# Hyena block with a gated FFN: gated values of twelve halves turned by way of memory and VectorE instead of TensorE

## Chip, cores and metric

One core of a Trainium2 chip runs the whole program. The metric is device time in microseconds, a median over runs; the profile is of one execution.

## The reference

Eight sequences of 512 positions with 512 features pass a long-convolution (Hyena) layer with a post-layernorm, then a gated FFN with quantised weights and a second post-layernorm.

```python
u = x @ in_proj_w.T + in_proj_b                      # (8, 512, 1536)
uc = short_conv(u, 3 taps, causal) + short_b         # per channel
x0, x1, v = split(uc, 3)                             # 512 channels each
v = v * x1                                           # the gated values
y = fftconv(v, k, filter_bias) * x0                  # long filter k from a small sine MLP
x = layernorm(x + y.T @ out_proj_w.T + out_proj_b)
h = silu(x @ Wg.T) * (x @ Wu.T)                      # 1408 hidden
out = layernorm(x + h @ Wd.T)
```

## The kernel before

The work is cut into 16 halves: half `n` is 256 of the 512 channels of sequence `n // 2` in the convolution part, and 256 of its 512 positions in the FFN part. The program is a software pipeline. Each round `n` has eleven beats (0 to 10), and in one round the engines work on the input projection (`ip`), short convolution (`conv`) and gating (`v1`) of half `n`, on the spectra and products of half `n-1` (`fw`, `mul`, `acc`, `iv`), on the output projection of half `n-2` (`op`, `ln1`), and on one FFN unit of 128 hidden features per beat (`gu`, `silu`, `hmul`, `hhi`, `hlo`, `dn`). A steady round takes about 60 us, a beat about 5.5 us. `beat_steps` writes the steps of a beat as a list, and every engine, SyncE with its DMA queue included, walks the same list in the same order and does its own part of each step. So each queue is strictly in order: an instruction that waits holds all that is behind it on its engine.

What the change and the prediction touch:

- **Gated values.** `v1` (GpSimd, L778) multiplies `cv` by `cx1` into `cv[:, c, :]`, channels on partitions, for channel blocks c = 0 and 1. In beats 7 and 8 the step `tv` (TensorE, L1094, four 128x128 products with the identity each) turns them to positions on partitions, into a PSUM bank; `vsplit` in the beat after copies the bank to `vT_hi` (ScalarE) and subtracts for `vT_lo` (VectorE, L899). `fw` of the next round reads both.
- **The ring of two banks.** `ip`, `tv`, `iv` and `op` take the two PSUM banks by turns. Each waits until the reader of the second last use is through. The second output projection of a round, `("op", n-2, 1)` in beat 7, takes the bank of the first one, which VectorE's `ln1` (L932) reads; `ln1` of beat 7 also waits for GpSimd's `resid` (L808).
- **SyncE's queue.** Beat 5: loading a block of down weights (`wdload`, L557), storing two blocks of the output (`store`, L623), and reloading `x` into their place (`resload`, L636), which waits until the stores have landed. In beats 1, 3, 5 and 7 of even rounds `xload` (L524) fetches a block of the next sequence in squares: four DMAs of 64 KB with runs of 128 bytes. VectorE turns these 32x32 squares (`xturn`, L863) in beats 2 to 5 of odd rounds. Beat 10: four DMA transposes (L614) from `parts` to `x2T_hi` and `x2T_lo`; `gu` of beat 2 in the next round waits for them.

Of the kernel before, what the change touches and what calls it, by code (L numbers as in the profile page):

```python
# [5 lines left out]
P = 128  # L6
NSEQ, L, D = 8, 512, 512
HID = 1408
TB = L // P
# [4 lines left out]
HALVES = 2 * NSEQ  # L14
# [44 lines left out]
BY_SQUARES = range(2, NSEQ)  # L59
SQUARE = 32  # L60


def shared(n, beat):

    ips, out, steps = n < HALVES, 0 <= n - 2 < HALVES, []
    if beat == 0 and 0 <= n - 3 < HALVES and n - 3 not in BY_DMA:
        steps += [("x2t", n - 3, 0), ("x2t", n - 3, 1)]
    if beat in (6, 7) and out:
        steps += [("op", n - 2, beat - 6)]
    if beat in PROJECTION_OF_BEAT and ips:  # L70
        steps += [("ip", n, *PROJECTION_OF_BEAT[beat])]
    if beat in (7, 8) and ips and n not in (1, 2):
        steps += [("tv", n, beat - 7)]
    if beat == 6 and n in (1, 2):
        steps += [("tv", n, 0), ("tv", n, 1)]
    if beat == 1 and out:
        steps += [("iv", n - 2, 3)]
    if beat in INVERSE_OF_BEAT and 1 <= n <= HALVES:
        steps += [("iv", n - 1, INVERSE_OF_BEAT[beat])]
    if beat in (9, 10) and n % 2 == 1 and n + 1 < HALVES and (n + 1) // 2 not in BY_SQUARES:  # L80
        steps += [("xt", (n + 1) // 2, 2 * (beat - 9) + b) for b in range(2)]
    return steps
# [15 lines left out]
def beat_steps(n, beat):  # L98
# [68 lines left out]
        steps += [("var", LN1, n - 2)]  # L167
    if beat in (9, 10):
        steps += readers([p for p in shared(n, beat) if p[0] == "xt"])
    following = (n + 1) // 2  # L170
    if n % 2 == 1 and following in BY_SQUARES:
        if beat in (2, 3, 4, 5):
            steps += [("xturn", following, beat - 2)]
        if beat in (7, 8, 9, 10):
            steps += [("xsplit", following, beat - 7)]
    if beat == 10 and n - 2 in BY_DMA:
# [128 lines left out]
def build(nc, x, win, wout, wg, wu, wd, fwd, shifted, inv, decay, z_pos, w0, w1, w2, w3, net_cols, fbias,  # L305
          conv_w, conv_cols, gate_cols, up_cols, down_row, out_row, identity, out):
    ctx = ExitStack()
    with ctx:
# [3 lines left out]
        def sem(name):  # L312
            return ctx.enter_context(nc.semaphore(name))
# [46 lines left out]
        spectrum = [ctx.enter_context(nc.psum_tensor(f"spectrum{n}", [P, 2, W], F32)) for n in range(2)]  # L360
        bank = [ctx.enter_context(nc.psum_tensor(f"bank{n}", [P, D], F32)) for n in range(2)]

        wd_scratch = nc.dram_tensor("wd_scratch", (HID, D), F32).ap()

        ident_in, consts_in, taps_in, late_in, decay_in = (sem(f"{n}_in") for n in ("ident", "consts", "taps", "late", "decay"))
# [21 lines left out]

        x_hi_done, x_lo_done, x_turned = sem("x_hi_done"), sem("x_lo_done"), sem("x_turned")
        tap2_done, tap1_done, v1_done = sem("tap2_done"), sem("tap1_done"), sem("v1_done")
        v_hi_done, z_hi_done, z_lo_done = sem("v_hi_done"), sem("z_hi_done"), sem("z_lo_done")  # L390
        res_biased, x2_hi_done, x2_lo_done = sem("res_biased"), sem("x2_hi_done"), sem("x2_lo_done")

# [10 lines left out]
        def flat(ap):  # L403
            return ap.rearrange("p a b -> p (a b)")
# [91 lines left out]
        def turned_block(kb):  # L496

            return xstage[:, kb - 1, :] if kb else turned[:, :]

        def by_dma(m):  # L500

            return min(max(m - BY_DMA[0], 0), len(BY_DMA))
# [7 lines left out]
        def _(sp):  # L510
# [77 lines left out]
            for kind, *at in steps:  # L588
# [8 lines left out]
                elif kind == "wdload":  # L597
                    m, q = at
                    index = HB * m + q
                    for n in ((0, 1, 2) if index == 0 else (index + 2,)):  # L600
                        if n < HB * HALVES:
                            load_down(n)
                elif kind == "x2dma":
                    m, = at
                    if m == BY_DMA[0]:
# [35 lines left out]
        def _(act):  # L641
# [13 lines left out]
            for kind, *at in steps:  # L655
# [29 lines left out]
                elif kind == "conv":  # L685
# [1 line left out]
                    q = COLS[t] * CB + 2 * (n % 2) + c  # L687
                    k = use["ip", n, c, t]
                    act.wait_ge(bank_ready, k + 1)
                    if t == V and n > 0:  # L690
                        act.wait_ge(bank_ready, use["tv", n - 1, 1] + 1)
                    elif t == X1:
                        act.wait_ge(v1_done, 2 * n + c)
                    elif t == X0 and n == 1:
                        act.wait_ge(filt_mm, 2 * TB)
                    elif t == X0 and n >= 2:
                        act.wait_ge(z_lo_done, TB * (n - 1))
# [6 lines left out]
                    last.then_inc(tap2_done, 1)  # L704
                elif kind == "vsplit":
                    n, jp = at
                    k = use["tv", n, jp]
                    act.wait_ge(bank_ready, k + 1)
                    if n > 0:
                        act.wait_ge(spectrum_ready, TB * (n - 1) + 2 * jp + 2)  # L710
                    A(flat(vT_hi[:, 2 * jp:2 * jp + 2, :]), bank_of(k), ACT.Copy).then_inc(v_hi_done, 1)
                elif kind == "z":
                    n, i = at
                    act.wait_ge(*read_of(use["iv", n, i]))
# [25 lines left out]
                elif kind == "x2part":  # L740
                    m, b = at
                    act.wait_ge(ln_done[LN1], 2 * m + b + 1)
                    if m > BY_DMA[0]:
                        act.wait_ge(x2t_in, 64 * by_dma(m))
                    A(parts[:, b, 0, :], row_tile(m, b), ACT.Copy).then_inc(x2_hi_done, 1)
# [74 lines left out]
        def _(dve):  # L820
# [5 lines left out]
            for kind, *at in steps:  # L826
# [55 lines left out]
                elif kind == "conv":  # L882
# [9 lines left out]
                    dve.wait_ge(tap1_done, number + 1)  # L892
                    STT(out=dst[:, 2:], in0=src[:, :L - 2], scalar=taps[:, q, 0:1], in1=dst[:, 2:],  # L893
                        op0=ALU.mult, op1=ALU.add).then_inc(bank_read[bank_index[k]], 1)
                elif kind == "vsplit":
                    n, jp = at
                    k = use["tv", n, jp]
                    dve.wait_ge(v_hi_done, 2 * n + jp + 1)
                    TT(flat(vT_lo[:, 2 * jp:2 * jp + 2, :]), bank_of(k), f32(flat(vT_hi[:, 2 * jp:2 * jp + 2, :])),  # L899
                       ALU.subtract).then_inc(bank_read[bank_index[k]], 1)  # L900
                elif kind == "mul":
# [101 lines left out]
        def _(pe):  # L1003
# [18 lines left out]
            for kind, *at in steps:  # L1022
# [74 lines left out]
                elif kind == "fw":  # L1097
                    n, j = at
                    k = TB * n + j
                    pe.wait_ge(*read_of(use["tv", n, j // 2]))  # L1100
                    if k >= 2:
                        pe.wait_ge(made_done, made["mul", n - (j < 2), (j + 2) % 4, 3, 1] + 1)
                    else:
# [133 lines left out]
```

## Time and profile before

| | us |
|---|---|
| median of 3 runs (lowest, highest) | 1011.18 (1010.74, 1011.89) |
| the profiled execution's own time | 1010.81 |
| its span | 1009.0 |
| PE busy | 988.4 |
| DVE busy | 733.8 |
| POOL busy | 570.6 |
| ACT busy | 425.8 |

The span runs from the first to the last instruction of the program; 1.8 us of the execution's time lie around it. PE is TensorE, DVE is VectorE, ACT is ScalarE, POOL is GpSimd, SPq is SyncE's queue, which issues the DMAs.

### The profile page before, as it was taken

How to read it: one execution, taken by the hardware profiler on the slowest of the kernel's cores; microseconds unless marked ns; L12 is line 12 of the kernel's file. 1: busy time of each engine (PE TensorE's matmuls, PEld its weight loads, DVE VectorE, ACT ScalarE, POOL GpSimd, SP SyncE). 2: the span in 40 equal slices, each digit the busy share in tenths (PEclk: the TensorE clock that was granted, in tenths of full speed). 3: DMA queues.
4: the chain of work that ended last, by engine and by line, in shares of the span. 5: the costliest groups of instructions: out<-in, count | busy, mean ns of one | idle time of the engine just before them, and what ended most of it. 6: DMA issues, size and time to landing. Idle time of an engine off the chain costs nothing.

```text
span 1009.0 us, 17595 instructions
## 1 busy us (share of the span) xinstructions
PE 988.4 (98%) x6214; PEld 803.3 (80%) x6214; DVE 733.8 (73%) x1338; ACT 425.8 (42%) x929; POOL 570.6 (57%) x628
## 2 busy tenths in 40 slices
PE   8999999999999999999999999999999999999996
PEld 5578788888888888888888888788888888888885
DVE  5598867868777787776878677876877777686454
ACT  4675434433343434434343343443334343434342
POOL 4599663756547465564647546465654746575210
PEclk9999999999999999999999999999999999999999
DMA  8674423242243413434223422424223231323332
GB/s 250 198 223 130 106 63 91 72 105 59 84 95 94 95 43 95 87 91 96 89 58 85 105 74 84 90 67 109 62 84 84 85 68 49 95 74 105 117 115 73
DMA packets 125883, 97.02 MB, mean 96 GB/s; under 512 B 83040, under 2 KB 87776, under 8 KB 125796
## 3 DMA queue, kind: packets, MB, share of 16 engines
q1 hardware_dynamic: 125298, 95.83, 35.3%
q8 instruction: 50, 0.82, 0.3%
q14 instruction: 37, 0.30, 0.1%
q10 hardware_dynamic: 498, 0.08, 0.0%
HBM read 78.30 MB, written 11.27 MB: 89 GB/s over the span
## 4 chain that ended last, share of the span: by engine, by line
PE 72%; DVE 13%; issue 6%; ACT 5%; SPq 2%; POOL 1%; DMA 1%; POOLq 0%; ACTq 0%; DVEq 0%
PE gate_up L1159 12%; PE gate_up L1160 12%; PE bank L1010 9%; PE bank L1012 9%; PE bank L1011 9%; PE down L1170 6%; PE down L1171 6%; PE bank L1119 4%; DVE tmp L917 2%; DVE hid_lo L1000 2%; ACT cx L702 2%; DVE cx L890 2%; ACT x L727 1%; PE bank L1094 1%; DVE cx L893 1%
## 5 line engine op out<-in xcount | busy, mean ns | idle before, releaser
L791 POOL TENSOR_TENSOR acc<-acc,tmp 128x256 f32<-128x256 f32 x160 | 123.0, 769 | 147.2 <-DVE tmp L917 135.1
L917 DVE TENSOR_TENSOR tmp<-spectrum,filt 128x512 f32<-128x512 f32 x256 | 173.0, 681 | 0.4 <-PE spectrum L1012 0.4
L755 ACT ACTIVATE hid<-gate_up,gate_scale 128x256 f32<-128x256 f32 x176 | 82.8, 471 | 197.6 <-PE gate_up L1160 196.5
L1159 PE MATMUL gate_up<-x2T_hi,wg_sb 128*128 128x256 f16 x704 | 165.0, 275 | 1.0 <-DMA x2T_lo<-parts 1.0
L1159 PE MATMUL gate_up<-x2T_hi,wu_sb 128*128 128x256 f16 x704 | 163.3, 273 | 0.0
L1160 PE MATMUL gate_up<-x2T_lo,wg_sb 128*128 128x256 f16 x704 | 163.2, 273 | 0.0
L1160 PE MATMUL gate_up<-x2T_lo,wu_sb 128*128 128x256 f16 x704 | 163.2, 273 | 0.0
L785 POOL TENSOR_TENSOR acc<-acc,tmp 128x512 f32<-128x512 f32 x96 | 126.4, 1317 | 48.5 <-DVE tmp L917 48.0
L1010 PE MATMUL bank<-xT_hi,win_hi 128*128 128x512 f32 x360 | 148.4, 412 | 0.8 <-POOL win_lo L773 0.6
L1170 PE MATMUL down<-wd_sb,hid_hi 128*128 128x512 f32 x352 | 148.7, 422 | 0.4 <-DVE hid_lo L1000 0.2
L1011 PE MATMUL bank<-xT_lo,win_hi 128*128 128x512 f32 x360 | 142.3, 395 | 0.0
L1012 PE MATMUL bank<-xT_hi,win_lo 128*128 128x512 f32 x360 | 142.1, 395 | 0.0
L1171 PE MATMUL down<-wd_sb,hid_lo 128*128 128x512 f32 x352 | 139.1, 395 | 0.0
L994 DVE SCALAR_TENSOR_TENSOR hid<-gate_up,up_scale,hid 128x256 f32<-128x256 f32 x176 | 84.4, 480 | 73.3 <-ACT hid L755 72.6
L1000 DVE TENSOR_TENSOR hid_lo<-hid,hid_hi 128x256 fp32r<-128x256 f32 x176 | 114.9, 653 | 28.5 <-ACT hid_hi L762 28.5
L762 ACT ACTIVATE hid_hi<-hid 128x256 fp32r<-128x256 f32 x176 | 73.6, 418 | 135.4 <-DVE hid L994 131.7
L792 POOL TENSOR_TENSOR acc<-acc,tmp 128x256 f32<-128x256 f32 x160 | 119.9, 749 | 0.0
L702 ACT ACTIVATE cx<-bank,conv_bias,taps 128x1 f32<-128x1 f32 x186 | 78.1, 490 | 95.9 <-PE bank L1012 92.6
L1159 PEld LDWEIGHTS gate_up<-x2T_hi,wg_sb 128*128 128x128 bf16 x704 | 68.5, 97 | 51.4 <-issue 43.6
L890 DVE SCALAR_TENSOR_TENSOR cx<-bank,taps,cx 128x511 f32<-128x511 f32 x62 | 46.2, 746 | 74.3 <-ACT cx L702 74.1
L1010 PEld LDWEIGHTS bank<-xT_hi,win_hi 128*128 128x128 f32 x360 | 67.8, 188 | 16.7 <-issue 2.0
L1012 PEld LDWEIGHTS bank<-xT_hi,win_lo 128*128 128x128 f32 x360 | 67.6, 188 | 16.3
(165 smaller groups left out, 1895.4 us busy)
## 6 DMA issues: line engine op xcount, KB each, us to landing
wd_sb<-wd_scratch SPq DMA_DIRECT2D x176, 256.0 KB, 2.7
x<-in_x SPq DMA_DIRECT2D x28, 256.0 KB, 2.7
out<-x SPq DMA_DIRECT2D x28, 256.0 KB, 3.2
xstage<-in_x SPq DMA_DIRECT2D x96, 64.0 KB, 2.9
xstage<-in_x SPq DMA_DIRECT2D x12, 256.0 KB, 4.0
x<-in_win SPq DMA_DIRECT2D x12, 256.0 KB, 5.0
acc<-in_decay SPq DMA_DIRECT2D x4, 256.0 KB
x<-in_wout SPq DMA_DIRECT2D x4, 256.0 KB, 2.8
```

Of the source, the lines that this page charges most:

```text
L785: G.tensor_tensor(acc[:, i, :, :], acc[:, i, :, :], temp_of(first), ALU.add).then_inc(temp_added, 1)
L791: G.tensor_tensor(acc[:, i, 0, :], acc[:, i, 0, :], t[:, 1, :], ALU.subtract)
L792: G.tensor_tensor(acc[:, i, 1, :], acc[:, i, 1, :], t[:, 0, :], ALU.add).then_inc(temp_added, 1)
L917: TT(dst, spectrum[j % 2][:, :, :], k_part, ALU.mult).then_inc(made_done, 1)
L1000: TT(hid_lo[:, k % 2, :], hid[:, k % 2, :], f32(hid_hi[:, k % 2, :]), ALU.subtract).then_inc(h_lo_done, 1)
L1010: mm(out_ap, ah, bh, start=k == 0, stop=False)
L1011: mm(out_ap, ah, bl, start=False, stop=False)
L1012: last = mm(out_ap, al, bh, start=False, stop=k == n - 1)
L1159: mm(dst, w[:, kb, rows(q)], x2T_hi[:, kb, ts], start=kb == 0, stop=False)
L1160: last = mm(dst, w[:, kb, rows(q)], x2T_lo[:, kb, ts], start=False, stop=kb == CB - 1)
L1170: mm(down[b][:, :], hid_hi[:, k % 2, rows(b)], wd_sb[:, k % 3, :], start=q == 0, stop=False)
L1171: last = mm(down[b][:, :], hid_lo[:, k % 2, rows(b)], wd_sb[:, k % 3, :], start=False, stop=q == HB - 1)
```

## The change

For halves 4 to 15 TensorE's `tv` is gone. In its place SyncE writes each `cv[:, c, :]` to memory as it stands (`vout`, 256 KB in runs of 512 bytes; c = 0 in beat 4, c = 1 in beat 6) and loads it back into `parts` in 32x32 squares that are already in their new places (`vback`, four DMAs of 64 KB each in runs of 128 bytes; c = 0 in beat 5, c = 1 in beat 6). VectorE turns the squares with one instruction for each c (`vturn`, beats 6 and 7), writing over `cv`. `vsplit` then reads SBUF in place of PSUM, in beat 9 and in beat 0 of the next round. `vturn` of c = 0 waits for both writes to memory, since it writes over both blocks, and for its own four loads. `xturn` moves to beats 0, 2, 2 and 6 of odd rounds.

```diff
+BY_MOVES = range(4, HALVES)
 def shared(n, beat):
-    if beat in (7, 8) and ips and n not in (1, 2):
+    if beat in (7, 8) and ips and n not in (1, 2) and n not in BY_MOVES:
         steps += [("tv", n, beat - 7)]
...
 def beat_steps(n, beat):
...
+    if n in BY_MOVES:
+        if beat in (4, 6):
+            steps += [("vout", n, beat // 2 - 2)]
+        if beat in (5, 6):
+            steps += [("vback", n, beat - 5)]
+        if beat in (6, 7):
+            steps += [("vturn", n, beat - 6)]
+        if beat == 9:
+            steps += [("vsplit", n, 0)]
+    if n - 1 in BY_MOVES and beat == 0:
+        steps += [("vsplit", n - 1, 1)]
     following = (n + 1) // 2
     if n % 2 == 1 and following in BY_SQUARES:
-        if beat in (2, 3, 4, 5):
-            steps += [("xturn", following, beat - 2)]
+        steps += [("xturn", following, kb) for kb in {0: (0, ), 2: (1, 2), 6: (3, )}.get(beat, ())]
...
+        v_scratch = nc.dram_tensor("v_scratch", (2, TB, P, P), F32).ap()
+        v_squares = flat(parts[:, 0, :, :].bitcast(F32)), flat(parts[:, 1, :, :].bitcast(F32))
+        v_turns = [cv[:, jp, :] for jp in range(2)]
...
@@ SyncE
+                elif kind == "vout":
+                    n, c = at
+                    sp.wait_ge(v1_done, 2 * n + c + 1)
+                    sp.wait_ge(v_in, 128 * by_moves(n))
+                    sp.dma_start(v_scratch[c].rearrange("t p i -> p t i"), cv[:, c, :].rearrange("p (t i) -> p t i", t=TB)).then_inc(v_out, 16)
+                elif kind == "vback":
+                    n, c = at
+                    sp.wait_ge(v_out, 32 * by_moves(n) + 16 * c + 16)
+                    sp.wait_ge(x2t_in, 64 * by_dma(n - 2))
+                    back = v_scratch[c].rearrange("t (b j) i -> j (t b) i", j=SQUARE)
+                    for a in range(P // SQUARE):
+                        cs = slice(a * SQUARE, (a + 1) * SQUARE)
+                        dst = v_squares[c][cs, :].rearrange("j (s i) -> j s i", i=SQUARE)
+                        sp.dma_start(dst, back[:, :, cs]).then_inc(v_in, 16)
...
@@ ScalarE
-                    if t == V and n > 0:
+                    if t == V and n - 1 in BY_MOVES:
+                        act.wait_ge(v_lo_done, 2 * by_moves(n))
+                    elif t == V and n > 0:
                         act.wait_ge(bank_ready, use["tv", n - 1, 1] + 1)
...
-                    k = use["tv", n, jp]
-                    act.wait_ge(bank_ready, k + 1)
+                    if n in BY_MOVES:
+                        act.wait_ge(v_turned, 2 * by_moves(n + 1))
+                        src = v_turns[jp]
...
@@ ScalarE, x2part
+                    act.wait_ge(v_turned, 2 * by_moves(m + 3))
...
@@ VectorE
+                elif kind == "vturn":
+                    n, c = at
+                    dve.wait_ge(v_out, 32 * by_moves(n + 1))
+                    dve.wait_ge(v_in, 128 * by_moves(n) + 64 * c + 64)
+                    turned_v = cv[:, :, :].rearrange("p a (t c) -> p (a t) c", c=W)[:, :, rows(c)]
+                    Vv.transpose(turned_v, v_squares[c]).then_inc(v_turned, 1)
...
+                    if n in BY_MOVES:
+                        TT(flat(vT_lo[:, 2 * jp:2 * jp + 2, :]), v_turns[jp], f32(flat(vT_hi[:, 2 * jp:2 * jp + 2, :])),
+                           ALU.subtract).then_inc(v_lo_done, 1)
+                        continue
...
@@ TensorE
-                    pe.wait_ge(*read_of(use["tv", n, j // 2]))
+                    if n in BY_MOVES:
+                        pe.wait_ge(v_lo_done, 2 * by_moves(n) + j // 2 + 1)
+                    else:
+                        pe.wait_ge(*read_of(use["tv", n, j // 2]))
```

The order on the queues that matter is shown at three places. First SyncE in an even round, beats 5 and 6 and on to the transfer of beat 7 (L524 and L546 are `xload`, L557 and L579 `wdload`, L623 and L660 `store`, L636 and L673 `resload`). Before:

```order
L623 DMA out<-x 128x512 [waits ln2_done] x2
L636 DMA x<-in_x 128x512 [waits stored0]
L636 DMA x<-in_x 128x512 [waits stored1]
L524 DMA xstage<-in_x 32x16x32 [waits x_lo_done]
L524 DMA xstage<-in_x 32x16x32 x3
L557 DMA wd_sb<-wd_scratch 128x512 [waits down_done] x2
```

After, the same stores first; L629 is `vout`, L639 `vback`:

```order
L660 DMA out<-x 128x512 [waits ln2_done] x2
L673 DMA x<-in_x 128x512 [waits stored0]
L673 DMA x<-in_x 128x512 [waits stored1]
L639 DMA parts<-v_scratch 32x16x32 [waits x2t_in,v_out]
L639 DMA parts<-v_scratch 32x16x32 x3
L546 DMA xstage<-in_x 32x16x32 [waits x_lo_done]
L546 DMA xstage<-in_x 32x16x32 x3
L579 DMA wd_sb<-wd_scratch 128x512 [waits down_done]
L629 DMA v_scratch<-cv 128x4x128 [waits v_in,v1_done]
L639 DMA parts<-v_scratch 32x16x32 [waits x2t_in,v_out]
L639 DMA parts<-v_scratch 32x16x32 x3
```

Between the reloads and `xload` of beat 5 there are four more DMAs, and after the down weights of beat 6 one write and four loads that wait for it.

Then VectorE at the end of beat 6 and the start of beat 7 in an odd round (L1000 and L1055 are `hlo`, L932 and L987 `ln1`, L890 and L935 the first tap of `conv`). Before:

```order
L917 TENSOR_TENSOR tmp<-spectrum,filt 128x512 [waits temp_added,spectrum_ready]
L1000 TENSOR_TENSOR hid_lo<-hid,hid_hi 128x256 [waits h_hi_done]
L932 TENSOR_TENSOR x<-bank,x 128x512 [waits res_biased,bank_ready]
L890 SCALAR_TENSOR_TENSOR cx<-bank,taps,cx 128x511 [waits tap2_done]
L893 SCALAR_TENSOR_TENSOR cx<-bank,taps,cx 128x510 [waits tap1_done]
```

After:

```order
L972 TENSOR_TENSOR tmp<-spectrum,filt 128x512 [waits temp_added,spectrum_ready]
L1055 TENSOR_TENSOR hid_lo<-hid,hid_hi 128x256 [waits h_hi_done]
L945 STREAM_TRANSPOSE cv<-parts 128x4x128 [waits v_in,v_out]
L908 STREAM_TRANSPOSE xstage<-xstage 128x512 [waits x_turned,x_in3]
L987 TENSOR_TENSOR x<-bank,x 128x512 [waits res_biased,bank_ready]
L935 SCALAR_TENSOR_TENSOR cx<-bank,taps,cx 128x511 [waits tap2_done]
```

`vturn` (L945) and the last `xturn` (L908) now stand ahead of `ln1`; in an even round `vturn` stands there alone.

Last TensorE at the end of the second output projection in beat 7. Before:

```order
L1010 MATMUL bank<-wout_hi,zb_hi 128x512
L1011 MATMUL bank<-wout_lo,zb_hi 128x512
L1012 MATMUL bank<-wout_hi,zb_lo 128x512
L1094 MATMUL bank<-ident,cv 128x128 [waits v1_done,bank_read1]
L1094 MATMUL bank<-ident,cv 128x128 x3
L1170 MATMUL down<-wd_sb,hid_hi 128x512 [waits wd_in0,h_lo_done]
L1171 MATMUL down<-wd_sb,hid_lo 128x512
```

After:

```order
L1065 MATMUL bank<-wout_hi,zb_hi 128x512
L1066 MATMUL bank<-wout_lo,zb_hi 128x512
L1067 MATMUL bank<-wout_hi,zb_lo 128x512
L1228 MATMUL down<-wd_sb,hid_hi 128x512 [waits wd_in0,h_lo_done]
L1229 MATMUL down<-wd_sb,hid_lo 128x512
```

The four transpositions between the output projection and the down projection are gone, as are the four of beat 8 ahead of `iv`.

## Rows read from the trace of the kernel before

**Rows 1.** The page: span, engines' busy time and share, granted TensorE clock.

```profile
span 1009.0 us, 17595 instructions
PE 988.4 (98%) x6214; PEld 803.3 (80%) x6214; DVE 733.8 (73%) x1338; ACT 425.8 (42%) x929; POOL 570.6 (57%) x628
...
PEclk9999999999999999999999999999999999999999
```

**Rows 2.** Waits on PE, 200 to 920 us: total us, times, longest.

```profile
PE bank L1010 <- DVE cx L893: 1.7, 6, 0.3
PE gate_up L1159 <- DMA x2T_lo<-parts: 1.0, 1, 1.0
```

**Rows 3.** Chain that ended last, around one transposition group: start us, us, what.

```profile
511.69 0.44 PE bank L1094 x4
```

**Rows 4.** SP's queue, round 8: start us, us, DMAs merged by line.

```profile
441.49 0.98 SPq L636 DMA_DIRECT2D x<-in_x  x2
442.51 2.03 SPq L524 DMA_DIRECT2D xstage<-in_x  x4
444.58 0.49 SPq L557 DMA_DIRECT2D wd_sb<-wd_scratch  x1
```

**Rows 5.** SP's queue, round 9, and the reloads of round 6.

```profile
322.00 2.19 SPq L636 DMA_DIRECT2D x<-in_x  x2
501.20 0.96 SPq L636 DMA_DIRECT2D x<-in_x  x2
502.21 0.43 SPq L557 DMA_DIRECT2D wd_sb<-wd_scratch  x1
```

**Rows 6.** DMA issues by line: count, KB each, median us to landing.

```profile
xstage<-in_x SPq DMA_DIRECT2D x96, 64.0 KB, 2.9
out<-x SPq DMA_DIRECT2D x28, 256.0 KB, 3.2
wd_scratch<-x2T_hi SPq DMA_DIRECT2D x4, 256.0 KB, 2.4
```

**Rows 7.** DVE in order of time, round 8: start us, us, work, idle before.

```profile
443.13 1.31 DVE L1000 TENSOR_TENSOR hid_lo<-hid,hid_hi 128x256 fp32r<-128x256 f32 x1
447.07 0.69 DVE L932 TENSOR_TENSOR x<-bank,x 128x512 f32<-128x512 f32 x1 [2.64 <-POOL x L808]
448.55 0.75 DVE L890 SCALAR_TENSOR_TENSOR cx<-bank,taps,cx 128x511 f32<-128x511 f32 x1 [0.79 <-ACT cx L702]
...
452.25 0.68 DVE L956 BATCH_NORM_STATS2 stats<-x 128x6 f32<-128x512 f32 x1
```

**Rows 8.** DVE in order of time, round 9.

```profile
503.03 1.30 DVE L1000 TENSOR_TENSOR hid_lo<-hid,hid_hi 128x256 fp32r<-128x256 f32 x1
```

**Rows 9.** PE in order of time, first matmul of the second output projection.

```profile
448.73 0.48 PE L1010 MATMUL bank<-wout_hi,za_hi 128*128 128x512 f32 x1
508.64 0.48 PE L1010 MATMUL bank<-wout_hi,za_hi 128*128 128x512 f32 x1
```

**Rows 10.** The transposition that VectorE does already: ns min/median/max.

```profile
L863 DVE STREAM_TRANSPOSE xstage<-xstage x18: 698/698/711, 128.0 to 737.2; 128x512 f32<-128x512 f32 x18
```

**Rows 11.** The way to the FFN: SP's transposes in rounds 8 and 9, shift, PE; L614's landing.

```profile
466.98 2.58 SPq L614 DMA_TRANSPOSE x2T_lo<-parts  x2
...
521.76 0.15 DVE L967 SCALAR_TENSOR_TENSOR shift<-moments,rstd 128x2 f32<-128x2 f32 x1
528.45 2.57 SPq L614 DMA_TRANSPOSE x2T_lo<-parts  x2
532.85 0.28 PE L1159 MATMUL gate_up<-x2T_hi,wg_sb 128*128 128x256 f16 x1
...
DMA to landing us min/median/max: 2.4/2.5/4.3
```

**Rows 12.** How long a reload holds SP: ns min/median/max.

```profile
L636 SPq DMA_DIRECT2D x<-in_x x28: 339/340/431, 55.7 to 861.7; - x28
```

**Rows 13.** Busy time after PE's last matmul: stretch, PE, ..., PEclk.

```profile
1000.00:1004.00 4.00, 0.01 (x1) 0.00 (x0) 3.84 (x9) 0.00 (x0) 0.00 (x0) 1.00 0.00 0
```

More of the change, by code:

```diff
@@ L389, in build @@
         tap2_done, tap1_done, v1_done = sem("tap2_done"), sem("tap1_done"), sem("v1_done")
+        v_out, v_in, v_turned, v_lo_done = (sem(n) for n in ("v_out", "v_in", "v_turned", "v_lo_done"))
         v_hi_done, z_hi_done, z_lo_done = sem("v_hi_done"), sem("z_hi_done"), sem("z_lo_done")
@@ L498, in turned_block, with by_moves @@
             return xstage[:, kb - 1, :] if kb else turned[:, :]
+        def by_moves(n):
+            return min(max(n - BY_MOVES[0], 0), len(BY_MOVES))
+        v_squares = flat(parts[:, 0, :, :].bitcast(F32)), flat(parts[:, 1, :, :].bitcast(F32))
+        v_turns = [cv[:, jp, :] for jp in range(2)]
         def by_dma(m):
@@ L706, in _ @@
                     n, jp = at
-                    k = use["tv", n, jp]
-                    act.wait_ge(bank_ready, k + 1)
+                    if n in BY_MOVES:
+                        act.wait_ge(v_turned, 2 * by_moves(n + 1))
+                        src = v_turns[jp]
+                    else:
+                        k = use["tv", n, jp]
+                        act.wait_ge(bank_ready, k + 1)
+                        src = bank_of(k)
                     if n > 0:
                         act.wait_ge(spectrum_ready, TB * (n - 1) + 2 * jp + 2)
-                    A(flat(vT_hi[:, 2 * jp:2 * jp + 2, :]), bank_of(k), ACT.Copy).then_inc(v_hi_done, 1)
+                    A(flat(vT_hi[:, 2 * jp:2 * jp + 2, :]), src, ACT.Copy).then_inc(v_hi_done, 1)
                 elif kind == "z":
@@ L894, in _ @@
                         op0=ALU.mult, op1=ALU.add).then_inc(bank_read[bank_index[k]], 1)
+                elif kind == "vturn":
[4 more added lines that the diff above has]
+                    Vv.transpose(turned_v, v_squares[c]).then_inc(v_turned, 1)
                 elif kind == "vsplit":
                     n, jp = at
+                    dve.wait_ge(v_hi_done, 2 * n + jp + 1)
+                    if n in BY_MOVES:
+                        TT(flat(vT_lo[:, 2 * jp:2 * jp + 2, :]), v_turns[jp], f32(flat(vT_hi[:, 2 * jp:2 * jp + 2, :])),
+                           ALU.subtract).then_inc(v_lo_done, 1)
+                        continue
                     k = use["tv", n, jp]
-                    dve.wait_ge(v_hi_done, 2 * n + jp + 1)
                     TT(flat(vT_lo[:, 2 * jp:2 * jp + 2, :]), bank_of(k), f32(flat(vT_hi[:, 2 * jp:2 * jp + 2, :])),
@@ L1099, in _ @@
                     k = TB * n + j
-                    pe.wait_ge(*read_of(use["tv", n, j // 2]))
+                    if n in BY_MOVES:
+                        pe.wait_ge(v_lo_done, 2 * by_moves(n) + j // 2 + 1)
+                    else:
+                        pe.wait_ge(*read_of(use["tv", n, j // 2]))
                     if k >= 2:
```

## Prediction

> **What bounds the kernel now.** I read the page first, then the waits, then the order of time on each engine in two neighbouring rounds. The page gives PE as busy for 988.4 of 1009.0 us, at the full clock in every slice [rows 1]. Between 200 and 920 us, where the pipeline is full, PE's waits for other engines come to a few us in all: 1.7 us for a bank and 1.0 us for a transfer to the FFN [rows 2]. So what is taken off PE is gained in full, if PE still waits for nothing. And the other way round: an engine that is late by more than its slack stops PE, and nothing gives that time back. The whole question is therefore what new lateness the detour brings, and at which of PE's waits.
>
> **What it removes.** Twelve rounds lose two groups of four transpositions. The chain of work charges a group with 0.44 us [rows 3]. That is 24 x 0.44 = 10.6 us. The profiled execution took 1010.8 us, 1.8 us of it outside the span, and the median is 0.4 us above that execution; the removal alone gives 1000.2 to 1000.6 us.
>
> **What it adds.** Two DVE transpositions for each round, 0.70 us each by those that DVE makes already [rows 10], 17 us in all on an engine with 275 us to spare [rows 1]. That sum says nothing; the place does. The two `vsplit` only change beat and source. SP gets two writes and eight loads a round. A load of 64 KB in squares holds SP for about 0.5 us: the four of `xload`, which have the same shape as the new ones, take 2.03 us [rows 4]. The bytes are no concern: 12 x 4 transfers of 256 KB, and the loads of that shape land in 2.9 us though they follow each other every half microsecond [rows 6].
>
> **Where it hurts: the first `vturn` of a round.** It waits for the write of c = 1, and that write is issued only in beat 6, behind everything that SP has in beats 5 and 6. On DVE it stands ahead of `ln1`, and `ln1` frees the bank for the second output projection. I follow this in both kinds of round.
>
> Round 8 (even). SP issues the reloads at 441.49 us, held until then by the landing of the stores, and is through with them at about 442.5. Now come four loads back (2.03), four of `xload` (2.03) and one block of down weights (0.49) [rows 4]: SP is at the write at 447.1. The write is new. The nearest rows are 256 KB to memory: `out<-x` lands 3.2 us after issue, `wd_scratch` 2.4 [rows 6]. I take 3.0, between them and nearer to the first, since it is the one measured in the full pipeline. So the write is there at 450.1. DVE has been free since 444.4, and before it took up `ln1` at 447.07 [rows 7]; now it does `vturn` (0.70) and `ln1` (0.69) and ends them at 451.5. PE wanted that bank at 448.73 [rows 9]. **Stall: 2.8 us.** Five even rounds (4, 6, 8, 10, 12) have `xload`: 14 us.
>
> The Trainium skill, "DMA: Bandwidth & Descriptors", section "Anatomy of one DMA", puts a DMA at about 2.0 us plus bytes over 436 GB/s. By that the write would land after about 2.6 us (an estimate from that page), and the sum over twelve rounds would be some 5 us smaller. The rows of this trace for the same size are longer for `out<-x`, and the measured ones decide.
>
> Round 9 (odd). Without `xload`, SP goes from the reloads straight to the loads back at 502.21 (2.03), the down weights (0.43) and the write at 504.7 [rows 5]. It lands at 507.7. DVE has been waiting since 504.33 and has to do `vturn`, the `xturn` that the change puts in beat 6, and `ln1`: 0.70 + 0.70 + 0.69, ready at 509.8, where PE came at 508.64 [rows 8, 9]. **Stall: 1.2 us**, in five odd rounds (5, 7, 9, 11, 13) 6 us. Rounds 14 and 15 have neither `xload` nor `xturn`: about 0.5 us each, 1 us.
>
> All this hangs on when the stores have landed. In round 6 the two reloads take 2.19 us instead of 0.96 [rows 5], since the second store is late, and rounds 5 and 7 look the same; that would shift the write by a further 1.2 us in three rounds, 3.6 us. It is chance which rounds are hit; I count half, 1.8 us.
>
> **What is late next.** Behind the stalled `vturn` stand `ln1`, the taps of `conv`, two products and `hmul`. Relative to PE they lose next to nothing, because DVE had idled 0.8 us for ACT ahead of the first tap [rows 7], and that idle time now goes. The second `vturn` needs the loads of c = 1, issued as soon as the write has landed: 1.5 us to the last issue and 2.9 us of landing, 4.4 us after the first `vturn` could start. DVE's own list up to there is `vturn` and `ln1` (1.4 us) and then all from the first tap to the end of the statistics, 448.55 to 452.93 in round 8 [rows 7], 4.4 us: 5.8 us together. No wait there. SP, held by this write for 3.0 us, has nothing urgent behind it: the down weights of beat 7 have to wait for PE's down projection of that beat anyway.
>
> One thing remains: the way to the FFN. In round 9 DVE makes the shift at 521.76, SP issues the last two of its four transposes from 528.45 to 531.02, one after the other, the last lands 2.5 us after its own issue at 529.7, and PE starts the product at 532.85 [rows 11]. That is 0.6 us of slack. PE now comes 0.88 us sooner after the output projection, and DVE's shift about 0.1 us later, since the first `vsplit` moves to just ahead of it in exchange for two that went. So PE waits about 0.4 us in each of the five odd rounds with such a transfer, 2 us. In even rounds there is no `xsplit` in the way: the last two transposes of round 8 start at 466.98, 18.3 us after the second output projection and not 19.8 as in round 9, so 2.1 us are left, and nothing happens [rows 9, 11]. The second `vsplit` and the `xturn` in beats 0 and 2 I cost at nothing: DVE is idle for 27% of the span [rows 1], and no wait of PE for DVE in those beats is near; without that cover they would cost their own 0.7 us each.
>
> **Sum.** 14 + 6 + 1 + 1.8 + 2 = 24.8 us of stalls, less 10.6: +14.2 us on 1010.8, that is **1025 us**. The kernel gets slower by 1.4%.
>
> **Bounds.** If the write lands in 2.4 us, 7 us less. If the loads back hold SP for 0.34 us each, as a reload does [rows 12], and not for 0.5, nearly 8 us less. If the write takes 3.6 us, since its runs are 512 bytes and it queues behind eight small loads, 7 us more; if the late stores come in every round, some 9 us more.
>
> **Rivals.**
> - *The write is there in time (faster).* The stall at `vturn` vanishes if the write lands 1.4 us before PE needs the bank: by 447.3 in round 8 and 506.5 in round 9, that is 2.8 and 1.2 us sooner than I have it. It takes a write of about 2 us in odd rounds and, in even ones, SP being through with eight loads in 1.9 us instead of 4.1. Then only the 10.6 us count, less some waits for the FFN: 1001 to 1004 us. Every row of SP speaks against it. 0.08.
> - *Gain and stall cancel.* Both lower bounds together, with the late stores gone, come out at 1009 to 1013 us. 0.05.
> - *PE's clock falls in the stalls.* In the kernel before, no wait is long enough to try it. After the last matmul the clock still stood at 1.00 through 4.0 us of idle PE [rows 13], and my longest stall is about 4 us in a round with a late store. If each of the five long ones cost 3 us of half clock, 1.5 us each would be added, and more if it stays low: 1032 to 1045 us. 0.07.
> - *The loads back are slow as a strided transposition.* The Trainium skill, "VectorE: DVE Perf Modes", section "The three transpose paths", warns that a plain DMA with the transposition in its strides is 19 times slower than the hardware's transposing DMA. As a mechanism here: the second `vturn` would wait for its loads, and each us that they take beyond 5 us after the first `vturn` goes to `ln1` and the statistics behind it, and from there into the way to the FFN, which has 0.6 us left in odd rounds. At 2 us of lateness that is some 10 us more, 1035. The loads of the same shape that land in 2.9 us [rows 6] speak against it: a run here is 128 bytes and DVE does the fine part. 0.06.
>
> The forecast has the remaining 0.74. The range, from the lower bounds one at a time with a few us more to the clock's first cases, is 1014 to 1037. Less than 0.2% either way (2 us) can't be told from no change here. From the cases: faster 0.08, same 0.03, slower 0.89.
>
> **What would show it.** The waits of PE should name `ln1` (through the bank) in front of the second output projection, once a round, near 3 us in even and 1 us in odd rounds, and the waits of DVE should name the write to `v_scratch` in front of the first `vturn`, with 5.7 us in even rounds and 3.4 in odd ones. SP's queue should show the write issued 5.6 us after the first reload in even rounds and 3.5 in odd ones. PE's busy time should fall by about 10 us, while the span grows. The prediction is wrong if the write is issued or lands much sooner than that, if PE's clock dips, or if the second `vturn` turns out to wait.

## The result and the profile after

The changed kernel takes 1059.95 us (median of 4 runs, 1059.5 to 1060.75) against 1011.09 us (median of 4) before: a ratio of 1.0484, 95% interval 1.0472 to 1.0497. It is 48.9 us slower, where I had forecast 14. The profiled execution has a span of 1058.3 us.

First the page of the kernel after, the lines that answer to [rows 1].

```profile
span 1058.3 us, 17597 instructions
PE 1001.2 (95%) x6118; PEld 806.0 (76%) x6118; DVE 750.3 (71%) x1362; ACT 424.8 (40%) x929; POOL 574.7 (54%) x628
...
PEclk9999999999999999999999899998999999999998
```

PE has 96 matmuls fewer and is busy for 13 us *longer*. Waits alone do little of that (twelve stalls at full clock, in the kernel with 9 statistics below, make PE's busy time 991.7 us, 3.3 more than before): the same matmuls must have run slower. The clock's line (`PEclk`, the granted clock of TensorE in 40 slices of the span) has three 8s where [rows 1] had only nines; the last of them lies in the idle end of the program. So two things are to be found, waits and clock.

The waits of the kernel after, on PE and on DVE (total us, times, longest):

```profile
PE bank L1065 <- DVE x L987: 36.9, 12, 4.4
...
DVE cv L945 <- DMA v_scratch<-cv: 72.4, 12, 7.6
```

Once in each of the twelve rounds PE waits for the bank that `ln1` (L987) reads, 36.9 us in all. In [rows 2] this wait did not exist. VectorE waits twelve times for the write to `v_scratch` in front of `vturn` (L945). Now round 8, first SP's queue in order of time, to be laid beside [rows 4]:

```profile
458.11 0.98 SPq L673 DMA_DIRECT2D x<-in_x  x2
459.19 3.42 SPq L639 DMA_DIRECT2D parts<-v_scratch  x4
462.66 2.08 SPq L546 DMA_DIRECT2D xstage<-in_x  x4
464.78 0.49 SPq L579 DMA_DIRECT2D wd_sb<-wd_scratch  x1
465.69 0.39 SPq L629 DMA_DIRECT2D v_scratch<-cv  x1
468.78 1.91 SPq L639 DMA_DIRECT2D parts<-v_scratch  x4
```

VectorE in the same round, in order of time with the idle time ahead of a row:

```profile
459.85 1.30 DVE L1055 TENSOR_TENSOR hid_lo<-hid,hid_hi 128x256 fp32r<-128x256 f32 x1
468.79 0.71 DVE L945 STREAM_TRANSPOSE cv<-parts 128x512 f32<-128x512 f32 x1 [7.64 <-DMA v_scratch<-cv]
469.42 0.65 DVE L987 TENSOR_TENSOR x<-bank,x 128x512 f32<-128x512 f32 x1
...
474.27 0.69 DVE L945 STREAM_TRANSPOSE cv<-parts 128x512 f32<-128x512 f32 x1
```

And TensorE, whose second output projection stands behind that `ln1`:

```profile
465.42 0.27 PE L1218 MATMUL gate_up<-x2T_lo,wu_sb 128*128 128x256 f16 x1
470.13 0.50 PE L1065 MATMUL bank<-wout_hi,za_hi 128*128 128x512 f32 x1 [4.44 <-DVE x L987]
...
471.17 0.63 PE L1065 MATMUL bank<-wout_hi,za_hi 128*128 128x512 f32 x1
471.60 0.63 PE L1066 MATMUL bank<-wout_lo,za_hi 128*128 128x512 f32 x1
472.02 0.63 PE L1067 MATMUL bank<-wout_hi,za_lo 128*128 128x512 f32 x1
```

The write is issued at 465.69 and lands at 468.8; `vturn`, `ln1` and the first matmul follow at once. PE idles for 4.44 us. Then look at the starts of the three matmuls from 471.17 on: they follow each other every 0.43 us. In round 9, on PE again, the same matmuls follow every 0.24 us:

```profile
533.08 0.50 PE L1065 MATMUL bank<-wout_hi,za_hi 128*128 128x512 f32 x1 [2.18 <-DVE x L987]
533.41 0.40 PE L1066 MATMUL bank<-wout_lo,za_hi 128*128 128x512 f32 x1
533.65 0.40 PE L1067 MATMUL bank<-wout_hi,za_lo 128*128 128x512 f32 x1
```

The windows behind the two stalls (stretch, length, busy time of PE, PEld, DVE, ACT, POOL, then PEclk) say why:

```profile
470.64:474.04 3.40, 3.40 (x9) 2.63 (x9) 3.36 (x7) 0.42 (x1) 1.71 (x2) 0.50 0.30 48
474.10:480.00 5.90, 5.90 (x44) 4.80 (x43) 4.06 (x9) 0.89 (x2) 3.08 (x5) 1.00 0.46 89
533.10:536.50 3.40, 3.40 (x15) 2.76 (x16) 3.36 (x6) 0.94 (x2) 1.30 (x1) 1.00 0.28 45
```

For 3.4 us behind the stall of round 8 the granted clock is 0.50, the lower of the two levels (1.2 GHz and not 2.4); then it is full again. Behind that of round 9 it stays full. There are eight such stretches in the trace, five of 3.4 us and three of 6.8, each at the end of one of the twelve stalls. They don't all begin behind it. In round 13 PE is idle from 789.36 to 792.49 us, and the clock falls 1.0 us before PE comes back:

```profile
789.40:791.40 2.00, 0.00 (x0) 0.00 (x0) 0.84 (x2) 0.47 (x1) 0.04 (x1) 1.00 0.35 107
791.50:792.40 0.90, 0.00 (x0) 0.00 (x0) 0.90 (x3) 0.00 (x0) 0.00 (x0) 0.50 0.73 116
792.60:798.30 5.70, 5.70 (x14) 4.44 (x15) 5.60 (x10) 0.94 (x2) 2.71 (x3) 0.50 0.15 24
```

The fall lies between 1.0 us before PE's return and 1.5 us behind it (round 7). The three stretches of 6.8 us are those of rounds 10, 12 and 13, in which it came 0.6 us or more before PE's return.

### The profile page after: what moved, and what is told of

It reads as the page before. It is cut to its first block, busy times and chain, and to the rows that moved or that the text cites. A ratio compares the mean times of both kernels' runs of the same rounds, so it can differ in the third digit from the quotient of the medians.

```text
span 1058.3 us, 17597 instructions
## 1 busy us (share of the span) xinstructions
PE 1001.2 (95%) x6118; PEld 806.0 (76%) x6118; DVE 750.3 (71%) x1362; ACT 424.8 (40%) x929; POOL 574.7 (54%) x628
## 4 chain that ended last, share of the span: by engine, by line
PE 54%; DVE 16%; DMA 9%; issue 8%; SPq 5%; ACT 5%; POOL 1%; ACTq 0%; POOLq 0%; DVEq 0%
PE gate_up L1217 9%; PE gate_up L1218 8%; PE bank L1065 7%; PE bank L1066 6%; PE bank L1067 6%; PE down L1228 5%; PE down L1229 4%; DMA out<-x 4%; DMA v_scratch<-cv 4%; DVE tmp L972 3%; PE bank L1177 3%; DVE hid_lo L1055 2%; SPq L639 2%; DVE hid L1049 2%; ACT cx L741 1%
## 5 line engine op out<-in xcount | busy, mean ns | idle before, releaser
L836 POOL TENSOR_TENSOR acc<-acc,tmp 128x256 f32<-128x256 f32 x160 | 123.6, 772 | 171.7 <-DVE tmp L972 160.6
L1055 DVE TENSOR_TENSOR hid_lo<-hid,hid_hi 128x256 fp32r<-128x256 f32 x176 | 112.9, 642 | 28.9 <-ACT hid_hi L807 28.9
L837 POOL TENSOR_TENSOR acc<-acc,tmp 128x256 f32<-128x256 f32 x160 | 123.4, 771 | 0.0
L935 DVE SCALAR_TENSOR_TENSOR cx<-bank,taps,cx 128x511 f32<-128x511 f32 x62 | 46.2, 745 | 65.4 <-ACT cx L741 65.3
```

Source lines behind the costliest of these rows:

```text
L836: G.tensor_tensor(acc[:, i, 0, :], acc[:, i, 0, :], t[:, 1, :], ALU.subtract)
L837: G.tensor_tensor(acc[:, i, 1, :], acc[:, i, 1, :], t[:, 0, :], ALU.add).then_inc(temp_added, 1)
L1055: TT(hid_lo[:, k % 2, :], hid[:, k % 2, :], f32(hid_hi[:, k % 2, :]), ALU.subtract).then_inc(h_lo_done, 1)
```

## The experiments

Theory A: the landing of the write of c = 1 holds VectorE, and through `ln1` the PE; the clock that falls in the longer stalls adds to it. Rival B: it is the traffic: 24 writes and 96 loads more, 12.6 MB in all by the pages, get in the way of other transfers. Rival C: the fall of the clock costs little, and the stalls explain it nearly all. In all kernels the numbers are medians, with the kernel before on the same chip beside them; one run where no interval is given.

**The write earlier** (e1). Both writes are issued in beat 4. Each c has semaphores of its own, so that the order of landing stays free.

```diff
-        if beat in (4, 6):
-            steps += [("vout", n, beat // 2 - 2)]
+        if beat == 4:
+            steps += [("vout", n, 0), ("vout", n, 1)]
...
```

> The changed kernel with one thing moved: the write of c = 1 to memory stands in beat 4 behind that of c = 0 (it then waits for the gating of c = 1), the loads back stay where they are; each c has semaphores of its own. Theory A (the first vturn waits for the write of c = 1, stops ln1 behind it and with it PE, and PE's clock falls in the long stalls): the write lands long before the first vturn, which now waits only for its own loads, landing about 6.1 us after the first output projection began. PE's stall before the second output projection falls from 3.8 to 4.4 us in even and 2.1 to 2.6 in odd rounds to about 0.1 and 0.7, no slice of the clock under 1, some 1.5 us of waits for the FFN's transfer: about 1006 us. Theory B (the added transfers, twice as many packets, slow the rest down wherever they stand): the stall may go, but the time stays above 1030 us.

Measured 1012.49 us against 1010.58, ratio 1.0020 (1.0010 to 1.0029). One step in one queue, moved by two beats, gives back 47 us, with every byte still transferred. The clock stays full while PE works. It is some 6 us worse than expected, and its waits say where:

```profile
PE bank L1068 <- DVE x L990: 3.7, 5, 0.9
...
DVE cv L948 <- DMA parts<-v_scratch: 38.1, 12, 4.1
```

The releaser of `vturn` is now the load back, not the write: those four loads stand behind the reloads, which wait for the stores. In five rounds (5, 8, 11, 13 and 15) that is still 0.4 to 0.9 us too late.

**`vturn` later** (e2). The transfers stay as changed; `vturn` moves to beats 7 and 8, behind `ln1`.

```diff
-        if beat in (6, 7):
-            steps += [("vturn", n, beat - 6)]
+        if beat in (7, 8):
+            steps += [("vturn", n, beat - 7)]
```

> The changed kernel with every transfer where it is, and the two vturn one beat later, at the end of beats 7 and 8, behind ln1. Theory A: the write still lands 8 to 10 us after the first output projection began, but nobody waits for it; no stall before the second output projection, clock full, the way to the FFN later by one transposition in odd rounds (up to 1 us each): about 1004 us. Theory B (traffic): above 1030 us.

Measured 1008.34 us against 1010.58, ratio 0.9982 (0.9973 to 0.9992). The write lands as late as before and nothing stalls at the output projection. What is late with no one waiting for it costs nothing. Of the expected gain 4 us are missing:

```profile
PE down L1228 <- DVE hid_lo L1055: 4.7, 11, 0.7
```

VectorE's work now comes in one stretch, and `hid_lo` in it is late for the down projection, up to 0.7 us.

**Clock and stall apart** (e3). The changed kernel, with 32 matmuls (16 in odd rounds and the last two) that nobody reads in PE's queue ahead of the second output projection of rounds 4 to 15.

```diff
+    if b == 1 and m + 2 in BY_MOVES:
+        at_unit = HB * (m - 1) + 5
+        pe.wait_ge(h_done, at_unit)
...
+        for f in range(32 if m % 2 == 0 and m + 2 < 14 else 16):
+            mm(gate_up[(at_unit + 1) % 2][:, 0, :], wg_sb[:, f % CB, rows(0)], x2T_hi[:, f % CB, ts], start=True, stop=True)
```

> The changed kernel, and PE makes matmuls whose result nobody reads, into the gate and up buffer that is free, just before it waits for the second output projection's bank: 32 of 256 columns (3.5 us) in even rounds 4 to 12, 16 (1.75 us) in the others. They are shorter than the stall, so the stall's end does not move. Theory A: the bank comes free as late as before, 37 us of stall remain in all (now mostly filled), but the clock stays at 1.00: about 1037 us, 23 us less than the changed kernel. If the clock's falls cost little and the rest of the loss is elsewhere (theory C: waits that are spread over the round): 1055 to 1060 us.

Measured 1043.04 us, where 1037 was expected: 16.9 us come back although PE does more work, and the clock is full in every slice. But the expectation's "the stall's end does not move" did not hold. From the first matmul of the round's first output projection to that of the second, the changed kernel takes 12.07 us in round 8 (458.06 to 470.13) and this one 11.71 (453.01 to 464.72); over the twelve rounds it is 4.8 us less. On SP the loads back went out sooner:

```profile
454.46 1.97 SPq L639 DMA_DIRECT2D parts<-v_scratch  x4
```

What lies between one round's second output projection and the next round's first is 13.8 us shorter in the eleven such stretches. That is the part in which the changed kernel has the half clock. At its two ends this kernel is 1.5 us slower. So C is refuted, but the clock's share is nearer to 14 us than to 16.9.

**`xload` out of the way** (e4). The `xload` of beat 5 moves behind the write, to the end of beat 6.

```diff
-        elif n > 2 and beat in (1, 3, 5, 7):
-            steps += [("xload", n // 2 + 1, beat // 2)]
+        elif n > 2 and beat in (1, 3, 6, 7):
+            steps += [("xload", n // 2 + 1, (1, 3, 6, 7).index(beat))]
```

> The changed kernel with the xload of beat 5 moved behind the loads back of beat 6 in even rounds, so that SP reaches the write of c = 1 four loads earlier. Theory A: the even rounds' stall falls from about 4.1 to about 2.1 us, as in odd rounds (8 to 10 us in five rounds), and with it most of the clock's falls, which lie in even rounds: about 1036 us. If the clock matters little: about 1051 us.

Measured 1040.26 us, 4 us more than expected. Taking 2.1 us out of SP's queue in five rounds takes 11.6 us out of the stalls, and 3 of the 8 falls of the clock with them:

```profile
PE bank L1065 <- DVE x L987: 25.3, 12, 2.6
```

The stalls are 1.4 to 2.6 us now, and the clock still falls at five of the twelve. One of the five is a stall of 1.8 us (round 14), while the longest, 2.6 us in round 15, was not followed by a fall.

**A stall without any detour.** The kernel before, with 9 (or 13, by `range(13)`) statistics that nobody reads on VectorE ahead of the first `ln1` of rounds 4 to 15. No transfer is added.

```diff
+    fwd_f32 = filt[:, 0, 0, :]
...
+    if b == 0 and 4 <= m + 2 < HALVES:
+        for f in range(9):
+            Vv.bn_stats(unread[:, m - 2, f, :], fwd_f32)
```

> The kernel before, its TensorE transpositions in place and no transfer added; in rounds 4 to 15 VectorE makes nine statistics of 512 columns whose result nobody reads, just ahead of the first ln1 (0.60 us each, of which 2.6 + 1.0 us are hidden). PE then waits 1.8 us before each of twelve second output projections, 22 us in all. If the clock falls only in stalls of some 3 us and more: about 1033 us. If it falls in these as well: 1040 to 1055 us.

> As the kernel with nine unread statistics, with thirteen: PE waits 4.2 us before each of twelve second output projections, 50 us in all. If the stall alone counts: about 1061 us. If the clock falls in each long stall and costs some 2 us each time, as 15 us for eight falls in the changed kernel say: about 1085 us, with twelve stretches at half clock.

With 9: 1031.2 us; the first wait below (total, times, longest), and a clock of 1.00 from 200 to 930 us. With 13: 1079.2 us; the second wait, and the window that holds the last 0.2 us of one of its stalls and 3.2 us behind it.

```profile
PE bank L1015 <- DVE x L937: 17.3, 12, 1.5
```

```profile
PE bank L1015 <- DVE x L937: 45.8, 12, 3.8
```

```profile
474.20:477.60 3.40, 3.21 (x8) 2.54 (x9) 3.36 (x7) 0.42 (x1) 1.15 (x1) 0.50 0.00 0
```

Four more statistics a round add 28.5 us of waits but 48 us of time. With 9, 20.3 us are lost for 17.3 us of waits, 0.25 us for each stall beyond its length. That is how a wait is counted. It begins at the end of the matmul ahead, and without a stall the next matmul starts before that end, as in the kernel before in round 8:

```profile
448.70 0.27 PE L1160 MATMUL gate_up<-x2T_lo,wu_sb 128*128 128x256 f16 x1
448.73 0.48 PE L1010 MATMUL bank<-wout_hi,za_hi 128*128 128x512 f32 x1
```

The second starts 0.24 us before the first has ended (at 448.97), and a stall takes that overlap too. With 13 statistics waits and overlap make 48.8 us of 68.3; the rest goes with the clock, at half in 11 stretches, three of them 6.8 us long. One of the twelve stalls of 3.8 us, that of round 4, was not followed by a fall. To see that rest by itself, the same kernel again with 32 unread matmuls in each stall:

> The kernel with thirteen unread statistics, and PE makes 32 unread matmuls (3.5 us) into the free gate and up buffer just before it waits for the second output projection's bank, in rounds 4 to 15. DVE's hold is unchanged, so the stall's end does not move. If the 1079.2 us of the kernel with thirteen are 50 us of stall and 18 us of half clock: 1061 us, no stretch at half clock. If the clock costs nothing: 1079 us.

Measured 1059.85 us. The second output projections start as late as before (11.4 to 11.5 us behind the first ones in every round of both), 19.3 us come back, and the clock is 1.00 throughout:

```profile
200.00:930.00 730.00, 722.85 (x4701) 594.12 (x4701) 605.23 (x1084) 275.58 (x609) 394.31 (x432) 1.00 0.30 78
```

A kernel with no added transfer comes out slower than the changed one, by one wait a round and the clock behind it.

**The moved `xturn` alone.** The kernel before, with only the line of `xturn` of the change.

> The kernel before with the change's one side edit alone: the xturn of odd rounds in beats 0, 2, 2 and 6 in place of 2, 3, 4 and 5. TensorE's transpositions stay and nothing is added. If the odd rounds' loss in beats 10 to 2 (1.35 us each in the kernel with everything early) comes from the added vturn and the moved vsplit, this changes nothing: 1010 to 1012 us. If it comes from the xturn in beats 0 and 6: about 1014 to 1017 us.

Measured 1009.83 us against 1011.07, ratio 0.9985 (0.9976 to 0.9994): it costs nothing, and rather gains 1.2 us.

**Everything of the transfer in beats 4 and 5** (e5). Both writes and the first loads in beat 4, the other loads in beat 5, so that no load of the first `vturn` stands behind the reloads. Semaphores for each c as in e1.

```diff
-        if beat in (4, 6):
-            steps += [("vout", n, beat // 2 - 2)]
-        if beat in (5, 6):
-            steps += [("vback", n, beat - 5)]
+        if beat == 4:
+            steps += [("vout", n, 0), ("vout", n, 1), ("vback", n, 0)]
+        if beat == 5:
+            steps += [("vback", n, 1)]
...
```

> The changed kernel with both writes and the first four loads back in beat 4 and the other four in beat 5; vturn and vsplit stay in beats 6, 7, 9 and 0. Theory A with the account of the runs so far: everything is in SBUF before DVE comes to the first vturn, which then fills the 2.6 us in which DVE waits for GpSimd ahead of ln1. No stall at the second output projection. Even rounds keep 0.86 us each. Odd rounds keep DVE's own lateness in beats 9 to 2 (a second transposition and the vsplit in a stretch where DVE is full): they gain 0.86 and lose 1.35 us there, minus what the first vturn no longer adds. 12 x 0.88 gained, 5 x 1 to 1.35 lost: 1005 to 1006 us. If the odd rounds' loss came from the stall alone: 1001 us.

Measured 1006.46 us against 1010.94, ratio 0.9956 (0.9942 to 0.9969). VectorE in round 9, in order of time:

```profile
500.81 1.30 DVE L1058 TENSOR_TENSOR hid_lo<-hid,hid_hi 128x256 fp32r<-128x256 f32 x1
502.04 0.70 DVE L948 STREAM_TRANSPOSE cv<-parts 128x512 f32<-128x512 f32 x1
502.67 0.66 DVE L910 STREAM_TRANSPOSE xstage<-xstage 128x512 f32<-128x512 f32 x1
504.76 0.69 DVE L990 TENSOR_TENSOR x<-bank,x 128x512 f32<-128x512 f32 x1 [1.43 <-POOL x L855]
...
517.82 0.67 DVE L1058 TENSOR_TENSOR hid_lo<-hid,hid_hi 128x256 fp32r<-128x256 f32 x1 [0.48 <-ACT hid_hi L809]
518.41 0.68 DVE L953 TENSOR_TENSOR vT_lo<-cv,vT_hi 128x512 fp32r<-128x512 f32 x1
```

`vturn` follows the row ahead of it without a pause, and `ln1` waits for `resid` on GpSimd as in [rows 7], with 1.43 us to spare. But two of PE's gaps behind the second output projection of this round are new, though small:

```profile
523.15 0.50 PE L1231 MATMUL down<-wd_sb,hid_hi 128*128 128x512 f32 x1 [0.22 <-DVE hid_lo L1058]
532.78 0.50 PE L1068 MATMUL bank<-xT_hi,win_hi 128*128 128x512 f32 x1 [0.28 <-DVE cv L940]
```

Of the 0.86 us that a round gains by its missing transpositions, even rounds keep about 0.7, and odd rounds end 0.49 us *later* than before (the 0.25 us that the moved `xturn` gives is not counted in).

**The same with `xturn` where it was.**

> The kernel with everything early, and the xturn of odd rounds back in beats 2, 3, 4 and 5. If the loss is that of vturn and vsplit: 1006 us as with the moved ones (beats 3 to 5 have idle DVE too). If the moved xturn cost it: about 1001 us.

Measured 1006.37 us against 1011.07, ratio 0.9953 (0.9937 to 0.9970): no clear difference to the run above. `xturn` is not what odd rounds lose by.

**The low parts behind the shift** (e6). As e5, and ScalarE's `vT_hi` of both c in beat 8, VectorE's `vT_lo` of both in beat 10 behind `norm`, where it no longer stands ahead of the shift.

```diff
-        if beat == 9:
-            steps += [("vsplit", n, 0)]
-    if n - 1 in BY_MOVES and beat == 0:
-        steps += [("vsplit", n - 1, 1)]
+        if beat == 8:
+            steps += [("vhi", n, 0), ("vhi", n, 1)]
+    if beat == 10 and n in BY_MOVES:
+        steps += [("vlo", n, 0), ("vlo", n, 1)]
```

> As the kernel with everything early, and the vsplit are taken apart: ScalarE makes both vT_hi at the end of beat 8, VectorE both vT_lo in beat 10 right behind the shift, where it idled 1.95 us for ScalarE in both kinds of round. If the odd rounds' loss is DVE's full stretch ahead of the shift and in beats 0 and 1 (theory A), the waits for the down projection in beat 10 and for the bank in beat 2 go, and the time is 1001 to 1003 us. If it is elsewhere, it stays with the other kernel's 1005.

Measured **999.75 us** (median of 4, 999.38 to 1000.46) against 1010.94, ratio 0.9888 (0.9874 to 0.9901). Even rounds keep all of the 0.87 us, odd ones 0.53, each without the moved `xturn`'s 0.25. This version beats both kernels and ends near the 1000.2 to 1000.6 us that I had worked out for the removal alone; what odd rounds still lose is made up by the moved `xturn` and by a wait for a transfer of 1.0 us, which the kernel before has in one round [rows 2] and this one has not.

B is refuted by e1, e2, e5 and e6 together: all of them make the same writes and loads as the changed kernel, and they take 999.75 to 1012.49 us.

## Why the prediction was wrong

It had the direction and the wait; the range missed by 23 us. Two steps failed. The term for the stalls was too small by 17 us, mostly by the time for which SP is held, and the fall of the clock, 14 us, was left out of the sum for a reason that does not bear it. The second is a failure of the mechanism and not only of a size: "if PE's clock dips" was one of the signs of being wrong. Point by point:

- **Removal, 10.6 us: right.** The rounds of the changed kernel run 0.86 us ahead by the end of beat 8, apart from their stalls: 10.3 us in twelve.
- **The stall, 22.8 us: right in kind, 39.8 us in size.** My 22.8 counted from the time at which PE had started on that bank; counted so, the twelve stalls are 36.9 us of waits and 2.9 us of lost overlap. In even rounds the waits are 3.8 to 4.4 us, where I had 2.8, in odd ones 2.1 to 3.1 (1.2), in the last two 2.0 to 2.1 (0.5). The failed step is "A load of 64 KB in squares holds SP for about 0.5 us". Of the four loads back in round 8, three do that, but the first holds SP for 1.83 us; the four together take 3.42 us, 2.65 to 3.74 in other rounds. In twelve rounds that is 11.7 us more than four times 2.03. The rest is 0.5 us of small gaps and 0.1 to 0.5 us more of landing. So in round 8 the write goes out 7.6 us after the first reload and not 5.6 (in round 9 4.3 and not 3.5), and lands 3.1 us later, near the 3.0 that I took. Over all 96 loads back (ns min/median/max):

```profile
L639 SPq DMA_DIRECT2D parts<-v_scratch x96: 312/488/2142, 203.6 to 918.2; - x96
```

Nor is this peculiar to the loads back. The rows of [rows 4] are of round 8, in which `xload` behind the reloads took 2.03 us; in round 4 of the same trace, at the same place, it took 3.50, its first load 1.84. The median hid what the longest one showed:

```profile
203.13 3.50 SPq L524 DMA_DIRECT2D xstage<-in_x  x4
```

The order on the queue alone does not decide it either. With the same order, the first load back was held over 1 us in eleven of twelve rounds of the changed kernel and in one of twelve with the unread matmuls (0.38 us in the others). No run shows the cause.
- **The clock, a rival at 0.07: it came.** "In the kernel before, no wait is long enough to try it" was true, and then I took the first 4 us of the idle end of the program [rows 13] as evidence that 4 us do no harm. The next stretch of the same trace shows the fall:

```profile
1004.00:1009.00 5.00, 0.00 (x0) 0.00 (x0) 0.71 (x2) 0.81 (x1) 0.69 (x1) 0.58 0.28 105
```

There PE's last matmul ended at 1000.0, and over the stretch from 1004 to 1009 us the clock is 0.58. In the trace after it was 1.00 through the 4.44 us of idle of round 8 and 0.50 only when PE was back at work. A full clock in an idle stretch says nothing of the clock behind it. All six stalls of 3.1 us or more came with half clock, and two of the six of 2.0 to 2.6 us. The cost: between one round's second output projection and the next round's first, the changed kernel is 14.0 us slower than e1, which has the same steps there and a full clock; in rounds 5, 9 and 14, without a fall, the two are within 0.01 us. The unread matmuls say 13.8 by the same measure. I had five falls at 1.5 us. There were eight: the stretches of 3.4 us cost 0.9 to 1.6 us each and the three longer ones 2.0 to 2.8.
- **Late stores, 1.8 us: did not occur.** The two reloads take 0.98 us in round 8, 0.94 in round 9 and 0.97 in rounds 5, 6 and 7, where I had looked for it. What I had called chance I should have left as a bound. (For late stores in every round I wrote 9 us more; 1.2 us in twelve rounds less the 1.8 counted are 12.6.)
- **Way to the FFN, 2 us in odd rounds: nothing there, but 5.7 us beside it.** No wait of PE names the transposes. Rounds 5, 7, 9 and 13 lose 1.35 us each behind the second output projection, at the down projection of beats 10 and 0 and at the input projection of beat 2 (round 11 loses 0.2). "The second `vsplit` and the `xturn` in beats 0 and 2 I cost at nothing" failed for `vsplit` and `vturn`: "DVE is idle for 27% of the span" is an average, and in an odd round VectorE has no idle time from the first tap of beat 7 until just before `hlo` of beat 10 (in e5 from 506.24 to 517.3). `xturn` costs nothing (two experiments); taking `vsplit` apart and moving `vT_lo` out of that stretch gives 6.7 us (e5 to e6).
- **The second `vturn` does not wait: right**; no wait of VectorE names it, and in round 8 it starts at 474.27 with no idle time ahead. **The transposition in strides is not slow: right**; the loads back land 2.4 us after issue (median, with a longest of 4.2).

The sum as measured: 39.8 us of stalls and 14.0 of clock. The rest is 4.5 us less than before: 10.3 by the removal and 1.1 by the moved `xturn`, against some 6.9 us lost, 5.7 of it in the odd rounds 5 to 13, 0.9 in even ones and the remainder in the last round. That makes 49.3 us, and the spans differ by 49.3 (1058.3 and 1009.0).

The Trainium skill's estimate for the write ("DMA: Bandwidth & Descriptors", section "Anatomy of one DMA"), 2.6 us, is shorter than the 3.1 to 3.5 us seen here. The page gives that fit for DMAs issued by GpSimd, and these are issued by SyncE. The measured landing of `out<-x` [rows 6] was the better guide.

Open: why the first load back holds SP for so long; and what, beside its length, decides whether a stall brings half clock: of two stalls of 2.2 us one (round 11) did and the other (round 9) did not. Also only argued: that `vturn` of c = 1 makes up what odd rounds still lose in e6, 0.3 us each at the down projection of beat 10; no run moved it alone. And the kernels with unread work (e3, with 9 and with 13 statistics) and e4 were timed once each.

## What to carry to other kernels

A detour that is cheap in bytes and busy time is priced by its first waiting instruction: find what stands behind it in its queue, work out when its producer can be issued in *its* queue, and place the issue as early as the data allow and the wait as late as the reader allows; here the place of a few steps in the list made the difference between 1060 and 1000 us. Where the sum gives PE stalls near 2 us or longer, count the clock with them: in the two kernels where it was measured it cost 35 to 40% of what the stalls cost (14.0 us beside 39.8, 19.3 beside 48.8). Unread matmuls in the stall are a quick way to measure it, if it is checked that the stall's end stays where it was. Full utilisation is read from the stretch in which an operation is put, not from the share of the span.

## What the runs showed that I had not expected

- The granted clock can stand at 1.00 through a whole stall of 4.4 us and fall when PE is back at work, for 3.4 us; in other stalls it falls up to 1.0 us before PE's return. Twelve stalls of 1.4 us never brought it down. The shortest that did was 1.8 us (e4), the longest that did not 3.8 us (13 statistics, round 4). One stretch of 3.4 us costs up to 1.6 us (matmuls every 0.43 and not every 0.24 us).
- Unread matmuls in a stall make a kernel faster: 1079.2 to 1059.85 us with the stalls unchanged, and 1059.95 to 1043.04 us with stalls that were 4.8 us shorter in sum.
- DMAs of one shape and size held SP for 0.49 us and for 1.83 us in the same group of four.
